# A four-layer graph network on one core: the dense-matrix steps of layer 0 take two source blocks in fp32 in place of four in three bf16 parts

## The reference

```python
h = relu(layernorm(x)); x = x + L0(h)   # segment_sum(relu(h[src] + edge_attr_16 @ We + be), dst), then a small MLP
h = relu(layernorm(x)); x = x + L1(h)   # 10 steps of h = 0.9 * segment_sum(h[s] * wn, d) + 0.1 * h0, wn from edge_weight and degrees
h = relu(layernorm(x)); x = x + L2(h)   # 3 attention layers over the edges
h = relu(layernorm(x)); x = x + L3(h)   # one edge convolution
```

## Time and profile before

| | |
|---|---|
| median of 3 runs | 4460.14 us |
| lowest, highest | 4458.2, 4472.35 us |
| span of the profiled execution | 4458.5 us |
| PE, DVE, POOL, ACT busy | 3158.4, 2785.2, 2993.2, 933.1 us |
| layer 0 with the dense steps | from 651 to 1364 us of the span |

### The profile page before, as it was taken

The page is one execution under the profiler, slowest core; times in us unless marked ns, Lnnn a source line. Parts: engine busy times, 40 slices in busy tenths (PEclk is TensorE's granted clock), DMA queues, the critical chain, the costliest instruction groups (busy, mean ns, idle before and its releaser), DMA issues.

```text
span 4458.5 us, 80594 instructions
## 1 busy us (share of the span) xinstructions
PE 3158.4 (71%) x19947; PEld 2109.2 (47%) x19958; DVE 2785.2 (62%) x10030; ACT 933.1 (21%) x3282; POOL 2993.2 (67%) x3059
## 2 busy tenths in 40 slices
PE   1240118888887999999678885888758788566665
PEld 1240004454443444343466664666646666445554
DVE  6970229998894111111688887888878888765554
ACT  0000003443341000000122222222212222112121
POOL 2677767777667888850377774777747777467776
PEclk9999999999997999999899997999979999755555
DMA  4310013333348999999322223222232222211112
GB/s 142 110 45 10 17 63 85 86 87 87 80 88 278 364 355 361 357 358 359 109 63 62 62 62 52 63 62 63 61 51 62 62 62 61 34 32 28 28 28 30
DMA packets 295308, 497.96 MB, mean 112 GB/s; under 512 B 165612, under 2 KB 210541, under 8 KB 293675
## 3 DMA queue, kind: packets, MB, share of 16 engines
q1 hardware_dynamic: 120119, 340.02, 21.7%
q0 software_dynamic: 92160, 115.39, 14.1%
q10 hardware_dynamic: 82800, 40.01, 3.1%
HBM read 435.66 MB, written 59.08 MB: 111 GB/s over the span
## 4 chain that ended last, share of the span: by engine, by line
PE 28%; POOL 25%; issue 19%; DMA 13%; DVE 10%; DVEq 1%; ACT 1%; SPq 1%; POOLq 0%; another core or an unknown queue 0%; ACTq 0%
PE ps L1545 26%; POOL arena L814 18%; DMA arena<-table,arena 10%; POOL rows_dst L797 7%; DMA rows_dst<-stage,arena 1%; DVE arena L1150 1%; DVE arena L1132 1%; PE ps L1730 1%; DMA arena<-in_edge_attr_dram 1%; DVE arena L1149 1%; DVEq L542 1%; DVE arena L1134 1%; DVE arena L1168 1%; DVE arena L1164 1%; DVE arena L1319 0%
## 5 line engine op out<-in xcount | busy, mean ns | idle before, releaser
L814 POOL DMA_INDIRECT arena<-table,arena x2080 | 2091.1, 1005 | 1104.3 <-issue 562.9
L1545 PE MATMUL ps<-arena 128*128 128x96 f32 (+3 forms) x9176 | 1473.3, 337 | 599.7 <-DVE arena L1168 252.4
L1545 PEld LDWEIGHTS ps<-arena 128*128 128x128 f32 (+3 forms) x9176 | 1025.4, 196 | 1017.5 <-issue 641.9
L1545 PE MATMUL ps<-arena,nodes 125*64 125x500 f32 (+2 forms) x3144 | 651.1, 538 | 33.4 <-DMA arena<-dense 22.8
L1150 DVE TENSOR_SCALAR arena<-iota_row_b,arena 128x128 f32<-128x128 bf16 x2080 | 579.9, 297 | 0.0
L768 POOL DMA_INDIRECT rows_src<-stage,stage_at x400 | 477.3, 1193 | 117.1 <-issue 109.3
L797 POOL DMA_INDIRECT rows_dst<-stage,arena x400 | 395.4, 989 | 223.3 <-issue 123.2
L1162 DVE TENSOR_TENSOR arena<-ps,arena 128x256 f32<-128x256 f32 x416 | 176.3, 424 | 531.6 <-DMA arena<-table,arena 516.4
L1149 DVE TENSOR_SCALAR arena<-iota_row_b,arena 128x128 bf16<-128x128 bf16 x1664 | 456.0, 276 | 2.1 <-DVE arena L1302 0.7
L1545 PEld LDWEIGHTS ps<-arena,nodes 125*64 125x64 f32 (+1 forms) x3144 | 242.6, 137 | 353.5 <-issue 321.1
L1251 DVE TENSOR_TENSOR nodes<-nodes,ps 125x256 f32 (+1 forms) x70 | 27.5, 392 | 608.4 <-PE ps L1730 608.4
(11 more groups left out here) (285 smaller groups left out, 3605.4 us busy)
## 6 DMA issues: line engine op xcount, KB each, us to landing
arena<-dense SPq DMA_DIRECT2D x240, 750.0 KB
nodes<-dense SPq DMA_DIRECT2D x60, 750.0 KB
dense<-arena ACTq DMA_DIRECT2D x150, 250.0 KB
arena<-table,arena POOLq DMA_INDIRECT x2080
arena<-dense SPq DMA_DIRECT2D x60, 500.0 KB, 7.7
arena<-rows_dst SPq DMA_DIRECT2D x208, 96.0 KB
arena<-dense SPq DMA_DIRECT2D x6, 2000.0 KB, 21.8
arena<-pair_rows SPq DMA_DIRECT2D x12, 976.6 KB
```

The source lines that it names most:

```text
L814: nc.gpsimd.indirect_dma_start(rows[:, u, k, 0:width], None, frm, bass.IndirectOffsetOnAxis(ap=p[:, c, j, c_other:c_other + 1].bitcast(I32 ...
L1545: return nc.tensor.matmul(to, lhsT, rhs, start=start, stop=stop, skip_group_check=True)
```

## The change

A dense step now takes `SB` = 2 source blocks, `SBW` = 250 columns. `lhs` is one fp32 operand of 128 columns with the weight as it is, `rhs` an fp32 one-hot of 250 columns, and PE does one fp32 product. The bins that ACT takes out are as before, 175 of up to four blocks: two sub-bins of 250 columns lie side by side in one bank. There are 13 sub-bins in a target block in place of 7 bins, so more tiles are visited twice: `PER_U` = (7, 7), 56 steps in a loop pass, 728 in all. The ring has 14 slots. The tables have 728 entries, and bank, column in the bank and count of bins come from columns worked out on DVE (`gone_*`) and summed on PE.

```diff
-PER2 = 11
-PER_U = (5, 6)
+SB, SBG = 2, 13
+SBW = SB * LO
+SBINS = HI * SBG
+SCH = -(-SBINS // LO)
+PER2 = 14
+PER_U = (7, 7)
...
-        lhs = carve([128, PER2, 3, 128], BF16)
-        rhs = carve([128, PER2, CW], BF16)
+        lhs = carve([128, PER2, 128])
+        rhs = carve([128, PER2, SBW])
...
-            for h, (b0, n) in enumerate(((0, LO), (LO, BINS - LO))):
+            for h, n in SBIN_CHUNKS:
+                b0 = h * LO
                 for x, first in enumerate((1, 1, 1, 0, 0)):
-                    sp.dma_start(bin_col[0:n, 2 * x + h:2 * x + h + 1],
+                    sp.dma_start(bin_col[0:n, SCH * x + h:SCH * x + h + 1],
...
-            for g in range(CG):
-                nc.vector.tensor_scalar(rel_key[:, g, :], src_blk, float(-g * CW), None, ALU.add)
-            for part in range(3):
-                link(nc.vector.tensor_copy(w_parts[:, :, part], w_left[:, part, :]))
-                if part < 2:
-                    link(nc.vector.tensor_tensor(w_left[:, part + 1, :], w_left[:, part, :], w_parts[:, :, part], ALU.subtract))
+            for g in range(SBG):
+                ins = nc.vector.tensor_scalar(rel_key[:, g, :], src_blk, float(-g * SBW), None, ALU.add)
+            link(ins)
...
                     v.wait_ge(built, i * PER_BODY + (first + k + 1))
-                    if (first + k) % 2:
-                        nc.vector.scalar_tensor_tensor(
-                            lhs[:, slot], iota_row_b[:].unsqueeze(1).to_broadcast([128, 3, 128]), lo_col[:, bass.ds(tile_at, 1)],
-                            w_parts[:, bass.ds(tile_at, 1), :].rearrange("p o c -> p (o c)").unsqueeze(2).to_broadcast([128, 3, 128]),
-                            ALU.is_equal, ALU.mult)
-                    else:
-                        for part in range(3):
-                            nc.vector.tensor_scalar(lhs[:, slot, part, :], iota_row_b[:], lo_col[:, bass.ds(tile_at, 1)],
-                                                    w_left[:, part, bass.ds(tile_at, 1)], ALU.is_equal, ALU.mult)
-                    nc.vector.tensor_scalar(rhs[:, slot, :], iota_col_h[:], flat_keys[:, bass.ds(key_at, 1)], None,
+                    nc.vector.tensor_scalar(lhs[:, slot, :], iota_row_b[:], lo_col[:, bass.ds(tile_at, 1)],
+                                            w_col[:, bass.ds(tile_at, 1)], ALU.is_equal, ALU.mult)
+                    nc.vector.tensor_scalar(rhs[:, slot, :], iota_col_h[:, 0:SBW], flat_keys[:, bass.ds(key_at, 1)], None,
                                             ALU.is_equal).then_inc(op_ready, 1)
...
-                    for part in range(3):
-                        ins = mm(flat[:, bass.ds(step_at["bank", first + k], CW)], lhs[:, slot, part, :], rhs[:, slot, :], start=False, stop=False)
-                    ins.then_inc(built, 1)
+                    mm(flat[:, bass.ds(step_at["bank", first + k], SBW)], lhs[:, slot, :], rhs[:, slot, :],
+                       start=False, stop=False).then_inc(built, 1)
```

More of the change, by code:

```diff
@@ L59 @@
 BINS = HI * CG
-PER2 = 11
-PER_U = (5, 6)
+SB, SBG = 2, 13
+SBW = SB * LO
+SBINS = HI * SBG
+SCH = -(-SBINS // LO)
+SBIN_CHUNKS = [(h, min(LO, SBINS - h * LO)) for h in range(SCH)]
+assert SBG == -(-HI // SB) and CB == 2 * SB and CG == -(-SBG // 2)
+PER2 = 14
+PER_U = (7, 7)
 PER_BODY = PER2 * U // 2
 STEPS_D = NB * PER_BODY
-TABLE_W = 576
-assert STEPS_D >= T - 1 + BINS - HI and STEPS_D <= TABLE_W and HI - (CG - 1) * CB == 1
+TABLE_W = STEPS_D
+assert STEPS_D >= T - 1 + SBINS - HI and TABLE_W <= 2 * 512 and HI - (CG - 1) * CB == 1
 EV = 2
@@ L233, in gnn_kernel @@
         iota_t = carve([128, TABLE_W])
-        bin_col = carve([128, 10])
+        bin_col = carve([128, 5 * SCH])
+        gone = carve([128, 2, SCH])
+        gone_d = carve([128, 2, SCH])
+        gone_g = carve([128, 2, SCH])
+        gone_pair = carve([128, 2, SCH])
+        gone_turn = carve([128, 2, SCH])
+        gone_need = carve([128, SCH])
+        gone_bank = carve([128, SCH])
         start_col = carve([128, 2])
-        bin_end_f = carve([1, BINS])
+        bin_end_f = carve([1, SBINS])
         tables_from = used[0]
-        begun = carve([128, 2, TABLE_W])
+        begun = carve([128, SCH, TABLE_W])
         bin_of = carve([1, TABLE_W])
@@ L302, in gnn_kernel @@
         src_all = carve([128, T])
[L303 to L305 removed]
+        w_col = carve([128, T])
+        rel_key = carve([128, SBG, T])
         assert used[0] <= KEEP_FROM
@@ L1063, in _, with down_by @@
-            for h, n in enumerate((LO, BINS - LO)):
+            def down_by(to, frm, n):
+                link(nc.vector.tensor_scalar(to, frm, 1.0 / n, -(0.5 - 0.5 / n), ALU.mult, ALU.add))
+                link(nc.vector.tensor_scalar(to, to, ROUND, None, ALU.add))
+                link(nc.vector.tensor_scalar(to, to, -ROUND, None, ALU.add))
+            for x in range(2):
+                for h in range(SCH):
+                    ins = nc.vector.tensor_scalar(gone[:, x, h:h + 1], iota_p[:], float(h * LO - x), None, ALU.add)
@@ new lines, in _ @@
+            link(ins)
+            down_by(gone_d, gone, SBG)
+            link(nc.vector.scalar_tensor_tensor(gone_g, gone_d, -float(SBG), gone, ALU.mult, ALU.add))
+            down_by(gone_pair, gone_g, 2)
+            link(nc.vector.scalar_tensor_tensor(gone_g, gone_pair, -2.0, gone_g, ALU.mult, ALU.add))
+            link(nc.vector.scalar_tensor_tensor(gone_d, gone_d, float(CG), gone_pair, ALU.mult, ALU.add))
+            down_by(gone_turn, gone_d, EV)
+            link(nc.vector.scalar_tensor_tensor(gone_turn, gone_turn, -float(EV), gone_d, ALU.mult, ALU.add))
@@ L1070, in step_sums @@
                 return ps[0:1, 2 * x:2 * x + 2, 0:TABLE_W // 2]
[L1072 to L1079, removed]
+            link(nc.vector.tensor_copy(need.rearrange(two, b=2), step_sums(0)))
+            link(nc.vector.tensor_scalar(bank_of.rearrange(two, b=2), step_sums(3), float(DB0 * 512 + (EV - 1) * 512), None, ALU.add))
+            for x, to, most in ((1, tile_of, T - 1), (2, key_of, SBG * T - 1)):
                 link(nc.vector.tensor_tensor(turn_of.rearrange(two, b=2), step_sums(x), iota_t[0:1, :].rearrange(two, b=2), ALU.add))
@@ L1584, in _ @@
             pe.wait_ge(here_ready, 3)
-            mm(s7[0:HI, 0:1], d_before[:, 0:HI], bin_incl[:, CG - 1:CG]).then_inc(summed, 1)
+            mm(s7[0:HI, 0:1], d_before[:, 0:HI], bin_incl[:, SBG - 1:SBG]).then_inc(summed, 1)
             pe.wait_ge(starts_ready, 1)
-            for x, column in enumerate((None, 2, 4)):
+            for x, weights in enumerate((gone_need, bin_col[:, SCH:2 * SCH], bin_col[:, 2 * SCH:3 * SCH], gone_bank)):
                 for half in range(2):
                     ts = slice(half * (TABLE_W // 2), (half + 1) * (TABLE_W // 2))
-                    for h, n in enumerate((LO, BINS - LO)):
-                        weights = one_each[0:n, 0:1] if column is None else bin_col[0:n, column + h:column + h + 1]
-                        ins = mm(ps[0:1, 2 * x + half, 0:TABLE_W // 2], weights, begun[0:n, h, ts], start=h == 0, stop=h == 1)
+                    for h, n in SBIN_CHUNKS:
+                        ins = mm(ps[0:1, 2 * x + half, 0:TABLE_W // 2], weights[0:n, h:h + 1], begun[0:n, h, ts],
+                                 start=h == 0, stop=h == SCH - 1)
             ins.then_inc(starts_summed, 1)
@@ L1607, in load4 @@
                 return load_values(pe, at_, lowest, highest)
-            step_at, fetch_steps = fours(pe, {"bank": (bank_of, DB0 * 512, (DB0 + EV - 1) * 512), "need": (need, 1, BINS)})
+            step_at, fetch_steps = fours(pe, {"bank": (bank_of, DB0 * 512, (DB0 + EV - 1) * 512 + SBW), "need": (need, 1, BINS)})
             at_least_one = pe.alloc_register("at_least_one")
```

44 lines of the change are left out of this document (26 added, 18 removed).

## The result

The changed kernel takes 4505.99 us (median of 4 runs, 4498.5 to 4513.49), the kernel before 4464.36 us beside it (4458.2 to 4472.35): a ratio of 1.0094, 95% interval 1.0076 to 1.0111. It is slower by 42 us; forecast were 14.

A forecast was written before the change was run, and what follows sets the result against it. DVE was taken as the bound before, PE's sequencer after: own time 663, ends 12, bank waits 32, long reads 20, sum 727 against 713 us, so 4460 + 14 = 4474 us, range 4430 to 4505.

The forecast's parts named there:

- VectorE: DVE in layer 0: `lhs` and `rhs` 0.26 us each, stage sum from 672 to 559 us, no longer the bound.
- The sequencer's own time: PE's sequencer in layer 0: 0.46 us a step, 111 us added, from 552 to 663 us, the longest sum.
- Waits for banks: PE's sequencer in layer 0: bank back after 2.6 us, bins of n steps cover (n + 1) x 0.46; 32 us.
- DVE's pace hid most of this, and 27.3 us showed.: Layer 0 before the change: DVE's pace hid most bank waits, and only 27.3 us of them showed.
- Ends and long reads: Layer 0: 12 us at the stage's two ends, and 20 us for table reads that take long.
- Setup: Ahead of layer 0: larger tables hidden by DVE's 84 us wait for scattered rows; 0 net, bounds -1 and +1.
- Case 1: Layer 0: the sequencer binds, with its waits; 4474 us, own range 4459 to 4490, chance 0.50.
- Case 2: Layer 0: the sequencer binds but waits shrink or steps issue quicker; 4435 to 4446 us, chance 0.17.
- Case 3: Layer 0: sequencer's time hides behind the array, DVE's relief counts; some 60 us less, near 4400, chance 0.10.
- case 4: Layer 0: fp32 `rhs` goes at one element per cycle, DVE needs 676 us; time 4497, chance 0.13.
- Case 5: Layer 0: less array work brings more stretches at 1.2 GHz; over 40 us, short dips nothing, chance 0.05.
- Case 6: Layer 0: gathers starve beside one-source DVE instructions, 1.66 us each; time 4560, chance 0.03.

The follow-up runs named there:

- run 10: Kernel before with its 572 steps of 500 columns kept, but one fp32 product in place of three bf16 ones: 4496.6 us, ratio 1.0099.
- Runs 5 and 6: Changed kernel, a bank taken out with one copy, three of four degree sums left out: 4488.7 us; the second also clears only 125 columns: 4478.0 us.
- run 8: Kernel before with a shorter eviction, one copy of 500 columns and three of the four degree sums left out: 4434.8 us, ratio 0.996.
- run 1: Changed kernel with one more wait, for a long-raised semaphore, on PE's sequencer before each of 728 dense steps: 4576.7 us, ratio 1.0264.
- run 11: Changed kernel with `lhs` and `rhs` in bf16 and a single product a step, weights losing their lower parts: 4505.3 us, ratio 1.0113.
- run 7: Changed kernel with one-copy eviction, clearing of 125 columns only, and the bank asked for only at every even step: 4464.6 us, ratio 1.0002.
- run 3: Changed kernel with a third one-hot of 128 columns, never read, on VectorE in each dense step: 4517.0 us, ratio 1.0128.
- run 9: Kernel before with the finer 728 steps of 250 columns, but still three bf16 products and their operands: 4559.1 us, ratio 1.0209.

## Why the prediction was wrong, by its own steps

- **VectorE.** Right. `lhs` and `rhs` follow each other by 0.26 us as taken, and the stage's busy time is 559 us. The reason given for `rhs`, half the elements of twice the size, isn't shown: in run 10 an fp32 `rhs` of 500 columns took 0.39, so half the columns save a third. Three rows in a row:

```profile
663.18 0.33 DVE L1156 TENSOR_SCALAR arena<-iota_row_b,arena 128x128 f32<-128x128 bf16 x1
663.44 0.33 DVE L1158 TENSOR_SCALAR arena<-iota_col_h,arena 128x250 f32<-128x250 f16 x1
663.70 0.33 DVE L1156 TENSOR_SCALAR arena<-iota_row_b,arena 128x128 f32<-128x128 bf16 x1
```

- **The sequencer's own time.** The step of 0.46 us and the addition of 111 us were right (107). The level was 29 us too high, 663 against 634; before it was 527, not 552.
- **Waits for banks: the step that failed.** Forecast 32 us, bounds 0 and 50; measured 79, outside them. The places were those foretold, their size was not. Not covered by a unit's end are 9 places with n = 1, mean 3.0 us (1.7 forecast), 6 with n = 2, 2.1 (1.2), and 34 with four or five steps, 26 us in all (30 x 0.3 = 9); covered ones, put at nothing, hold another 11. The term that was too small is the time in which a bank comes back: 3.7 us on average for a full bank, not 2.6. The eviction is 1.75 as read from the earlier trace rows; but from the issue of a bin's last step until the second half of its product starts it takes 0.94 (median 0.58), and from there to the first copy another 1.00 (median 0.58), 1.9 in all where I had 0.9 for "a product's drain and two hand-overs". The 47 us that were missing have three sources:
  - *The usual case, 18 us.* With both delays at their medians a bank comes back after 2.9 us, and the 49 uncovered places would hold 50 us; I had 32. Part of it is that from the issue of the last step the sequencer's own work covers 0.68 us at n = 1 and 1.17 at n = 2, where I took 0.92 and 1.38.
  - *A slow array, 17 us.* The 49 places hold 66 us. Of the 17 above the usual case, 14 stand at nine places where the last step ran in a stretch at 1.2 GHz or up to 2 us behind one; there it lay 2.0 us in the queue, at the other 40 places 0.7.
  - *Places put at nothing, 12 us*, most of them through ScalarE's own queue. At the start of each target block it reads seven ends of bins, and the first copy comes 2.65 us behind the product (median of 25 bins; 0.58 at the four-block bins behind it). At four of its loop turns it comes 4 to 5.4 us behind, more than a unit's end covered: these four places hold 7.4 us. One such read, and the copy behind it:

```profile
L562 ACTq TENSOR_LOAD <-arena x1: 1687/1687/1687, 810.9 to 810.9; - x1
```
```profile
814.48 0.28 ACT L1449 ACTIVATE arena<-ps 128x125 f32<-128x125 f32 x1 [3.90 <-issue]
```

Runs 5 and 6 show the size of the loop: 0.46 and 0.77 us less eviction take 25 and 36 us off the holds.
- **"DVE's pace hid most of this, and 27.3 us showed."** Wrong. These are stops of the array; the sequencer held 101 us for banks in the kernel before, and the array's queue hid a part of it only: run 8 shows that it cost time there too.
- **Ends and long reads.** 7 us against 12, and some 24 against 20. Another 16 us are waits of other kinds, which the forecast didn't have.
- **The sum.** 663 + 12 + 32 + 20 = 727 us; measured 634 + 7 + 79 + 24 + 16 = 760. Of the 33 us between, 47 are bank holds, 20 smaller waits, and -34 own time and ends that I had too high. So the level of the own time, wrong the other way, hid 29 us of the miss.
- **Setup.** Not shown either way: the time ahead of the stage varies by 8 us from run to run, more than the change could have moved it.
- **Rivals.** Case 1 is the mechanism, with waits larger than its range. Case 2 needed waits and ends below 37 us; they were 126. Case 3 is ruled out by the result, a longer stage with DVE relieved, and by run 1, case 4 by the 0.26 us. Case 5: the granted clock fell from 0.97 to 0.92 in the stage (44 us at 1.2 GHz in 12 stretches before, 120 in 27 after), as feared, and short dips were not free: they account for the 14 us of holds above, an estimate from the 49 places. The case itself needed over 40 us and a clock below 0.9. Case 6: gathers got shorter (1045 ns on average in place of 1225); the one-source instructions that took the place of L1126 didn't starve them.
- **What would show it.** Issue stops, step distance and VectorE's busy time came as listed. "PE's waits on DVE vanish" did not by the profile's rows: they rose from 32.8 to 51.4 us, because it files holds for banks under this name. By the sequencer's records they did, from 47 to 8 us.

**Still open:** what run 11 would take at the changed kernel's clock, and so how much the length of the product is worth; and how much of run 7's remaining 95 us of holds is the early asking. Whether a third bank would lift the holds, wasn't tried.

## What to carry to other kernels

Add up the sequencer of an engine as you add up its datapath: here more but lighter instructions freed the busiest engine and made the issuing side the bound. Where a few buffers go round between engines, a hold adds to the issuer's own time at each turn; measure the whole way round from issue to release at many places, the usual case and the slow ones (here 18 and some 29 of the 47 us that the forecast missed). And a wait that the profile gives to an engine with less work than before may belong to something issued ahead of it: look at the issuer's rows at one such place. Last, a run that takes work off the array can lower its clock: split its steps by the granted clock before you read it as a test of the work alone.

## What the runs showed of the hardware that I had not expected

**Less work for the array, a lower clock, the same time.** With a single bf16 product a step (run 11) the granted clock in the stage was 0.68, 488 of 758 us at 1.2 GHz, with one fp32 product of 500 columns (run 10) 0.99. The stage of run 11 was as long as the changed kernel's at 0.92. That is not because a lower clock is free where the sequencer sets the pace: in or just behind a stretch at 1.2 GHz a step waited 0.92 us for the array in run 11, elsewhere 0.14, and the holds behind bins of a single step were 3.1 and 1.7 us. The shorter product made up for it.

**Gathers take longer or shorter with what VectorE runs beside them.** From 700 to 1300 us, changed kernel and run 3:

```profile
L827 POOL DMA_INDIRECT arena<-table,arena x334 | 348.9, 1045 | 251.5 <-DMA arena<-rows_dst 151.3 <-issue 87.3 <-DMA arena<-table,arena 12.6
```
```profile
L828 POOL DMA_INDIRECT arena<-table,arena x335 | 479.7, 1432 | 124.2 <-issue 87.6 <-DMA arena<-rows_dst 20.1 <-DMA arena<-table,arena 15.9
```

With the wide left side of two inputs (L1126) in every second step a gather took 1225 ns, and 1144 in run 9; without it 1045, 977 in run 10 and 976 in run 11. But 728 more one-source one-hots (run 3) brought it to 1432. The Trainium skill, SBUF — State Buffer (SBUF: two separate sides), says that VectorE in a two-port mode, or with two SBUF inputs against an instruction of GpSimd that reads SBUF, and GpSimd exclude each other from a shared port pair. The numbers with and without L1126 go that way, and run 3's would if its one-hots ran in such a mode, which no row shows. That it is this lock wasn't tried, and a rival is open: VectorE was also busy for 88 to 91% of the stage in the three kernels with long gathers, and for 63 to 74% in the three with short ones.
